# Two attention layers in one step loop: one row of maxima per quad, scores three steps behind

## The chip, the cores and the metric

One core of one Trainium2 chip. The metric is the time of one execution in device microseconds, the median of the runs shown; a change of some 0.2% is about the least that can be told.

## The reference, cut to what matters

Eight batches of 256 tokens with 256 features go through four layers, each added to x: cross-attention with a mask (called A here), a quantised linear layer, cross-attention with a bias and a feed-forward part (called C here), and a mixture of eight experts. Both attentions have 16 heads of 16 features; keys and values come from a context that is the same for A and C.

```python
x = x + _L0_xattn_ref(_layernorm(x), ctx, ctx, mask, W, b)          # A: scores, mask, softmax, values, W
x = x + _L0_ffn_ref(_layernorm(x), weight)                          # hadamard, 4-bit activations, ternary weight
x = x + _L1_xattn_ref(_layernorm(x), ctx, bias, Wq, Wk, Wv, ...)    # C: softmax(q k / 4 + bias) v, Wo, gelu FFN
x = x + _L1_ffn_ref(_layernorm(x) ..., Wr, W1, b1, W2, b2)          # top-k experts
```

The softmax is exact in form: the largest score of each row is taken away before the exponential.

## The kernel before, in words

**Quads.** The 16 heads of a batch are worked in four *quads* of four heads, of kind A or C. A quad's scores are 4 heads x 256 x 256. It has two *halves* of two heads. Each half is computed twice on TensorE, since the maximum has to be known first: once with queries along the partitions (`pe_maximum_scores`, L435, into the PSUM tile `row_scores`), of which VectorE takes the maximum of each row (`ve_take_maximum`, L646: one reduction for A, four fused add-and-maximum instructions with the bias for C), and once with keys along the partitions (`pe_scores`, L451, into `key_scores`), ready for the product with the values. Between the two, the maxima are laid into `row_max`, transposed on TensorE (`pe_maximum_rows`, L502, one pair of 128x128 transposes for each half, into `ps_r`) and added by VectorE to spare rows of the query operand (`ve_add_maximum`, L665, 64 partitions for each half), so that the second product gives scores with the maximum taken away. For A the mask is put in by two matmuls ahead of each product (`pe_mask`, L456). For C VectorE adds the bias to `key_scores` into `probs` (`ve_add_bias`, L677). ScalarE then takes the exponentials (`ac_exponentials`, L832), GpSimd sums blocks (`po_sum_blocks`, L968), and after both quads of a *chunk* TensorE forms the values and the row sums (`pe_values`, L511, into `ps_v`), which VectorE divides (`ve_normalise`, L687).

**Order of the work.** `timetable` (L52) puts each quad at a position. From the third batch on, A quads of batch b stand at even positions and C quads of batch b - 2 at odd ones, so A and C alternate; the first two batches have A quads alone, and the last two C quads stand side by side. Each position has two *steps*, one for each half, and a batch has 16 steps. In step 2p + h every engine does, in its own order: the maxima of half h of the quad at p + 1 (`then`), the scores of half h of the quad at p (`now`), the transposes and the add for the maxima of the step before, at h = 1 the values and the division of the quad before (where it ends a chunk), then the side jobs that a table puts at that step. Both products of a step are woven into one *round* (`pe_round`, L459): the two halves use different 32-row strips of the array (`group`, L372), so four matmuls run side by side. A round waits for the maxima of the step before to be taken (one `row_scores`), for `key_scores` to be read (by ScalarE for A, by VectorE for C) and for `max_added` of the half whose scores it forms. Where both quads are C, the two products go one behind the other (`pe_scores_apart`, L483); in this timetable that is so in the last two batches alone.

**Side jobs.** `PE_SLOT`, `VE_SLOT`, `AC_SLOT`, `PO_SLOT` (L87 to L96) give the step of each other piece of a batch, relative to 16 b; `move` (L106 to L121) overrides them for single batches. The names: T_x transposes a LayerNorm result, wa/wo the output products of A and C, had, T_q, tern the quantised layer, wk, wq, wv the projections of C, f1_n and f2_n the feed-forward parts, lg the router's logits; on VectorE st and ap are the LayerNorm statistics and their application, on GpSimd rs the reciprocal root, on ScalarE g0, g1 the gelus. The engines are in order; semaphores join them. SyncE's queue issues all loads in one loop over positions (L1465).

```python
for step in range(2 * FIRST, 2 * LAST):
    pos, half = divmod(step, 2)
    now, then, past = quad_of(pos), quad_of(pos + 1), quad_of(pos - 1)
    maximised, of_half = previous_half(step)
```

After the attention steps come the router (VectorE, `ve_route`, `ve_threshold`) and the eight experts.

## Time and profile before

| | |
|---|---|
| median of 3 runs | 979.02 us (977.69 to 979.81) |
| profiled execution | 979.38 us, its span 977.6 us |
| granted TensorE clock, mean | 0.921 |
| PE, DVE, ACT, POOL busy | 86%, 68%, 40%, 47% of the span |
| attention steps | first round at 13.67 us, last logits of the last batch copied at 712.59 us |

PE is TensorE's matmuls, PEld its weight loads, DVE VectorE, ACT ScalarE, POOL GpSimd, SP SyncE. Busy time of PE is modelled at its ends, so two neighbours can overlap by some 0.1 us; the distance from start to start is exact. A gap in square brackets is idle time of that engine ahead of the instruction, with what ended it.

### The profile page before, as it was taken

Reading aid. Unit: us, or ns where it says so; the run is one execution under the profiler, and the core shown is the slowest. Engines: PE = TensorE matmul, PEld = TensorE weight load, DVE = VectorE, ACT = ScalarE, POOL = GpSimd, SP = SyncE. Lnnn points to the kernel's source line nnn. Section 1 sums busy time; section 2 is a strip of 40 time slices with the busy share of each in tenths; the row PEclk is TensorE's granted clock in tenths of the full one; section 3 lists DMA queues with packets and bytes.
Section 4 is the critical chain, followed back from the end, with each engine's and each line's share of the span. In section 5 each row is a group of like instructions: output and inputs, shape, how many; then the busy total and the mean of one; then the engine's idle time right before and its main releaser. Section 6 shows DMA issues by size and latency. Waiting matters only on the chain.

```text
span 977.6 us, 17867 instructions
## 1 busy us (share of the span) xinstructions
PE 841.3 (86%) x7077; PEld 608.6 (62%) x7077; DVE 663.2 (68%) x1501; ACT 387.9 (40%) x594; POOL 456.9 (47%) x403
## 2 busy tenths in 40 slices
PE   6888877989999999999999979998733499999995
PEld 4555444545665665665665656666622399999985
DVE  4664468787798798798698687683266466666441
ACT  1322122324624624624524413423110266666662
POOL 4444234544536536536435334152320467777742
PEclk9998789989999999999999978989955599999998
DMA  9320543443443443443443335240050135545531
GB/s 288 123 61 12 199 167 131 141 150 109 149 164 117 160 168 115 161 168 112 159 140 112 127 129 195 91 148 11 33 183 0 44 114 130 135 130 130 135 71 22
DMA packets 47696, 120.57 MB, mean 123 GB/s; under 512 B 4736, under 2 KB 33920, under 8 KB 39424
## 3 DMA queue, kind: packets, MB, share of 16 engines
q1 hardware_dynamic: 41472, 111.06, 33.5%
q0 software_dynamic: 6144, 8.39, 4.8%
q8 instruction: 56, 0.92, 0.4%
q14 instruction: 24, 0.20, 0.1%
HBM read 111.05 MB, written 8.39 MB: 122 GB/s over the span
## 4 chain that ended last, share of the span: by engine, by line
PE 59%; DVE 21%; issue 7%; POOL 6%; ACT 4%; DMA 1%; POOLq 0%; SPq 0%; DVEq 0%
PE row_scores L437 9%; PE ps_v L525 8%; PE row_scores L1289 5%; PE ps_m L543 4%; PE ps_v L1306 4%; PE ps_r L1306 4%; DVE probs L683 3%; DVE row_max L653 3%; PE ps_v L407 3%; PE ps_m L414 3%; PE ps_r L507 2%; DVE attnT_C L692 2%; PE key_scores L457 2%; PE key_scores L1289 2%; PE ps_m L535 2%
## 5 line engine op out<-in xcount | busy, mean ns | idle before, releaser
L972 POOL TENSOR_TENSOR probs<-probs 128x512 f32<-128x512 f32 x128 | 162.0, 1272 | 112.2 <-ACT probs L841 89.4
L841 ACT ACTIVATE probs<-probs 128x1024 f32<-128x1024 f32 x64 | 67.7, 1057 | 233.1 <-DVE probs L683 233.0
L660 DVE CUSTOM_DVE_ANT_0 row_scores<-row_scores,bias_q 128x256 f32<-128x256 f32 x256 | 100.6, 453 | 38.3 <-PE row_scores L437 38.1
L838 ACT ACTIVATE probs<-key_scores 128x1024 f32<-128x1024 f32 x64 | 65.6, 1025 | 125.6 <-PE key_scores L453 124.9
L653 DVE TENSOR_REDUCE row_max<-row_scores 128x4 f32<-128x1024 f32 x64 | 78.1, 1221 | 48.3 <-PE row_scores L437 48.2
L683 DVE TENSOR_TENSOR probs<-key_scores,bias_k 128x1024 f32<-128x1024 f32 x64 | 77.8, 1215 | 7.5 <-PE key_scores L453 7.3
L437 PE MATMUL row_scores<-k_op_a,q_op_A 32*128 32x256 f32 x512 | 77.1, 420 | 6.4 <-DVE q_op_C L669 5.9
L437 PE MATMUL row_scores<-k_op_c,q_op_C 32*128 32x256 f32 x512 | 75.3, 413 | 4.9 <-DVE row_max L660 4.9
L453 PE MATMUL key_scores<-q_op_C,k_op_c 32*128 32x256 f32 x512 | 77.9, 424 | 0.4 <-DVE q_op_C L669 0.4
L453 PE MATMUL key_scores<-q_op_A,k_op_a 32*128 32x256 f32 x512 | 74.8, 411 | 0.0
L1371 POOL TENSOR_TENSOR w_l<-w1e,w_h 128x512 fp32r<-128x512 f32 x32 | 52.4, 1668 | 42.6 <-ACT w_h L1322 42.6
L1239 DVE TENSOR_TENSOR hid_l<-hid_e,hid_h 128x512 fp32r<-128x512 f32 x64 | 44.3, 692 | 40.8 <-ACT hid_e L1340 40.8
L437 PEld LDWEIGHTS row_scores<-k_op_a,q_op_A 32*128 32x128 f32 x512 | 47.1, 193 | 37.4 <-issue 22.0
L1380 POOL DMA_INDIRECT out<-y_g,idx x32 | 54.0, 1688 | 28.0 <-ACT y_g L1354 18.2
L437 PEld LDWEIGHTS row_scores<-k_op_c,q_op_C 32*128 32x128 f32 x512 | 45.0, 189 | 32.5 <-issue 17.9
L543 PE MATMUL ps_m<-w,hidT 128*128 128x256 f32 x256 | 61.0, 381 | 0.0
L1363 POOL DMA_INDIRECT xg<-normed_dram,idx x32 | 37.5, 1171 | 49.6 <-DVE idx L1213 36.0
L507 PE MATMUL ps_r<-ident,row_max 128*128 128x128 f32 x256 | 58.4, 311 | 0.0
L457 PE MATMUL row_scores<-mask_bf,ident_b 128*128 128x512 bf16 x128 | 40.1, 397 | 19.4 <-DVE row_max L653 11.0
L507 PEld LDWEIGHTS ps_r<-ident,row_max 128*128 128x128 f32 x256 | 26.6, 145 | 46.0 <-issue 46.0
L543 PEld LDWEIGHTS ps_m<-w,hidT 128*128 128x128 f32 x256 | 47.4, 190 | 6.6 <-issue 0.8
L453 PEld LDWEIGHTS key_scores<-q_op_C,k_op_c 32*128 32x128 f32 x512 | 46.9, 194 | 4.9 <-issue 2.4
(242 smaller groups left out, 2160.0 us busy)
## 6 DMA issues: line engine op xcount, KB each, us to landing
bias_q<-in_bias_q SPq DMA_DIRECT2D x32, 1024.0 KB, 5.0
bias_k<-in_bias_k SPq DMA_DIRECT2D x32, 1024.0 KB, 5.0
w1e<-in_w1e SPq DMA_DIRECT2D x8, 1024.0 KB, 5.1
w2e<-in_w2e SPq DMA_DIRECT2D x8, 1024.0 KB, 6.7
k_op_a<-in_k_a SPq DMA_DIRECT2D x32, 128.0 KB, 2.3
mask_int<-in_mask SPq DMA_DIRECT2D x8, 512.0 KB, 5.7
v_op_A<-in_v_a SPq DMA_DIRECT2D x8, 512.0 KB, 5.4
w<-in_w SPq DMA_DIRECT2D x2, 1024.0 KB, 10.4
```

Of the source, the lines that this page charges most:

```text
L437: return nc.tensor.matmul(row_scores[:, j % 2, qt * SEQ:(qt + 1) * SEQ], queries(q)[r, qt * P:(qt + 1) * P], keys(q)[r, :], start=(q.kind ...
L453: return nc.tensor.matmul(key_scores[:, j % 2, kb * SEQ:(kb + 1) * SEQ], keys(q)[r, kb * P:(kb + 1) * P], queries(q)[r, :], start=(q.kind ...
L507: ins = nc.tensor.matmul(ps_r[:, qt * P:(qt + 1) * P], row_max[q.par][MAX_TILE[q, half]][:, qt, :], ident[:, :], start=True, stop=True, is ...
L525: ins = nc.tensor.matmul(bank[32 * j:32 * j + 32, col:col + SEQ], left, probs[:, (first, last)[par] % 4, j, kb, :], start=(par == 0 and kb ...
L543: ins = nc.tensor.matmul(ps_m[1][:, t * D:(t + 1) * D], hidT[:, hc, t * P:(t + 1) * P], w_2[:, hc, :], start=(t == 0 and hc == 0), stop=(l ...
L653: nc.vector.tensor_reduce(of, row_scores[:, :, :].rearrange("p j (t k) -> p j t k", t=QT), AX_X, ALU.max).then_inc(max_taken, 1)
L660: ins = nc.vector.tensor_tensor_reduce(row_scores[:, j, qt * SEQ:(qt + 1) * SEQ], row_scores[:, j, qt * SEQ:(qt + 1) * SEQ], bias_q[:, m % ...
L683: nc.vector.tensor_tensor(probs[:, n % 4, heads(q, half), :, :].rearrange("p j t q -> p j (t q)"), key_scores[:, :, :], bias_k[:, m % 2, h ...
L841: nc.scalar.activation(of, of, ACT.Exp).then_inc(exp_done, 1)
L972: nc.gpsimd.tensor_tensor(both[:, :, 0, :], both[:, :, 0, :], both[:, :, 1, :], ALU.add).then_inc(blocks_summed, 1)
L1289: ins = nc.tensor.matmul(ps_h[hc % 3][:, :], w[:, c, cols_h], xT[:, c, :], start=(n == 0), stop=(n == 3 * DC - 1))
L1306: ins = nc.tensor.matmul(ps_e[i][:, (st % 2) * D:(st % 2 + 1) * D], hid[:, hc, st * P:(st + 1) * P], w[:, hc, :], start=(n == 0), stop=(n ...
```

## The change: what it does

Maxima stay where they are (`maximised_at`: the quad at p + 1 in steps 2p and 2p + 1). The transposes and the add are made once for a whole quad, in the even step after both its halves (`rows_at`); `row_max` has two tiles for each parity in place of three. The scores of a quad at p come at steps 2p + 1 and 2p + 2 (`scored_at`), one step later than before, and the values one step later (`valued_at`, always at an even step). Halves are strips 0 and 1 for every quad. C with C goes as a whole round except in the last two batches. The side jobs get new steps; in the tail every one is a step later.

```diff
-MAX_TILE = {(q, half): (2 * [p for p in ORDER if p.par == q.par].index(q) + half) % 3 for q in ORDER for half in range(2)}
...
 def values_step(kind, b, c):
-    return 2 * values_place(kind, b, c) + 1
-PE_SLOT = {"wb": -5, "wa": 0, "T_A": -32, "wv": 18, "wo": 35, "T_B": 3, "had": 4, "T_F": 39, "T_q": 6, "tern": 8, "f1_0": 40,
-           "T_R": 58, "f1_1": 42, "lg": 59, "f1_2": 43, "wk": 12, "T_C": 13, "f1_3": 45, "wq": 14,
-           "f2_0": 46, "f2_1": 50, "f2_2": 52, "f2_3": 53, "f2_4": 53, "f2_5": 53, "f2_6": 54, "f2_7": 54}
-VE_SLOT = {"wb0": -10, "wb1": -9, "wb2": -8, "wb3": -7, "stA": -35, "mask": -32, "apA": -34, "x1": 0, "apB": 2, "y": 35,
-           "quant": 4, "qcap": 5, "apF": 37, "yf": 54, "apG": 55, "yq": 8, "stR": 56, "apR": 57, "stC": 10, "apC": 11,
-           "lgc": 59}
-AC_SLOT = {"wb": -5, "qA": -32, "vC": 18, "hbT": 3, "zT": 39, "qT": 6, "xrT": 58, "g0": 42, "kC": 12, "xcT": 13, "g1": 45,
-           "qC": 14}
-PO_SLOT = {"rsA": -35, "xb": -34, "rsB": 0, "rsF": 35, "yb": 37, "rsG": 54, "aff": 55, "x2": 8, "rsR": 56, "rsC": 10,
-           "xe": 12, "mk": -21}
+    return 2 * PLACE[Quad(kind, b, 2 * c + 1)] + 4
+PE_SLOT = {"wb": -4, "wa": 1, "T_A": -30, "wv": 19, "T_B": 4, "had": 5, "wo": 38, "T_F": 41, "T_q": 7, "tern": 8, "f1_0": 43,
+          "wk": 11, "f1_1": 44, "T_C": 13, "f1_2": 45, "wq": 14, "f1_3": 46, "T_R": 63, "lg": 64,
+           "f2_0": 47, "f2_1": 49, "f2_2": 51, "f2_3": 52, "f2_4": 52, "f2_5": 53, "f2_6": 54, "f2_7": 55}
+VE_SLOT = {"wb0": -10, "wb1": -9, "wb2": -8, "wb3": -7, "stA": -35, "mask": -32, "apA": -34, "x1": 1, "apB": 3,
+           "quant": 5, "qcap": 6, "y": 38, "yf": 55, "apF": 39, "yq": 9, "apG": 57, "stR": 59, "stC": 11, "apC": 12, "apR": 61,
+           "lgc": 65}
+AC_SLOT = {"wb": -4, "qA": -30, "vC": 19, "hbT": 4, "zT": 41, "qT": 7, "kC": 11, "g0": 44, "xcT": 13, "qC": 14, "g1": 46,
+           "xrT": 63}
+PO_SLOT = {"rsA": -35, "xb": -34, "rsB": 1, "rsF": 38, "yb": 39, "rsG": 55, "x2": 9, "aff": 57, "rsR": 59, "rsC": 11,
+           "xe": 13, "mk": -20}
...
-move(0, stA=-32, rsA=-32, apA=-31, xb=-31, T_A=-30, qA=-30, wa=2, x1=2, rsB=2, apB=2, T_q=5, qT=5, qcap=4, tern=6, yq=6,
...
+move(0, stA=-32, rsA=-32, apA=-31, xb=-31, T_A=-30, qA=-30, wa=3, x1=3, rsB=3, apB=3, T_B=4, hbT=4, had=5, quant=5, qcap=5,
...
-move(4, f2_0=111, f2_1=111, f2_2=112, f2_3=112, f2_4=112, f2_5=113, f2_6=113, f2_7=113, yf=114, rsG=114, apG=115, aff=115,
...
+move(4, f2_0=112, f2_1=112, f2_2=113, f2_3=113, f2_4=113, f2_5=114, f2_6=114, f2_7=114, yf=115, rsG=115, apG=116, aff=116,
...
-        row_max = [[lay(f"row_max_{par}{n}", [P, QT, P]) for n in range(3)] for par in range(2)]
+        row_max = [[lay(f"row_max_{par}{n}", [P, QT, P]) for n in range(2)] for par in range(2)]
...
-        def group(quad, half):
-            return (PLACE[quad] - 1 + half) % 2
-
-        def previous_half(step):
-            pos, half = divmod(step - 1, 2)
-            return quad_of(pos + 1), half
+        def maximised_at(step):
+
+            return quad_of(step // 2 + 1), step % 2
+
+        def scored_at(step):
+            return quad_of((step - 1) // 2), (step - 1) % 2
+
+        def rows_at(step):
+            return quad_of(step // 2) if step % 2 == 0 else None
+
+        def valued_at(step):
+            q = quad_of(step // 2 - 2) if step % 2 == 0 else None
+            return q if q is not None and q.par == 1 else None
...
             nc.tensor.matmul(bank, ident_b[:, :], mask_bf[:, q.b % 2, way, :], start=True, stop=False)
 
-        def pe_round(pe, now, then, half):
+        def pe_round(pe, now, of_now, then, of_then):
             if then is not None:
-                pe_wait_maximum(pe, then, half)
+                pe_wait_maximum(pe, then, of_then)
                 if then.kind == A:
                     for n in range(2):
                         pe_mask(row_scores[:, n, :], then, 0)
             if now is not None:
-                pe_wait_scores(pe, now, half)
+                pe_wait_scores(pe, now, of_now)
                 if now.kind == A:
                     for n in range(2):
                         pe_mask(key_scores[:, n, :], now, 1)
-                pe.wait_ge(max_added, half_number(now, half) + 1)
+                pe.wait_ge(max_added, number(now) + 1)
...
-        def pe_maximum_rows(pe, q, half):
-            n = half_number(q, half)
-            pe.wait_ge(max_taken, n + 1)
-            wait(pe, max_added, n)
+        def pe_maximum_rows(pe, q):
+            pe.wait_ge(max_taken, 2 * number(q) + 2)
+            wait(pe, max_added, number(q))
             for qt in range(QT):
-                ins = nc.tensor.matmul(ps_r[:, qt * P:(qt + 1) * P], row_max[q.par][MAX_TILE[q, half]][:, qt, :], ident[:, :],
+                ins = nc.tensor.matmul(ps_r[:, qt * P:(qt + 1) * P], row_max[q.par][MAX_TILE[q]][:, qt, :], ident[:, :],
                                        start=True, stop=True, is_transpose=True)
...
             for step in range(2 * FIRST, 2 * LAST):
-                pos, half = divmod(step, 2)
-                now, then, past = quad_of(pos), quad_of(pos + 1), quad_of(pos - 1)
-                maximised, of_half = previous_half(step)
-                if now is not None and then is not None and now.kind == then.kind == C:
-                    pe_scores_apart(pe, now, then, half)
+                (now, of_now), (then, of_then) = scored_at(step), maximised_at(step)
+                if now is not None and then is not None and now.kind == then.kind == C and now.b >= NB - 2:
+                    pe_scores_apart(pe, now, of_now, then, of_then)
                 elif now is not None or then is not None:
-                    pe_round(pe, now, then, half)
-                if maximised is not None:
-                    pe_maximum_rows(pe, maximised, of_half)
-                if half == 1 and past is not None and past.par == 1:
-                    pe_values(pe, past)
+                    pe_round(pe, now, of_now, then, of_then)
+                if rows_at(step) is not None:
+                    pe_maximum_rows(pe, rows_at(step))
+                if valued_at(step) is not None:
+                    pe_values(pe, valued_at(step))
                 for job, b in due(PE_SLOT, step):
...
 
-        def ve_add_maximum(ve, q, half):
-            g = group(q, half)
-            r = slice(64 * g, 64 * g + 64)
-            ve.wait_ge(max_rows, half_number(q, half) + 1)
-            nc.vector.tensor_tensor(queries(q)[r, :], ps_r[r, 0:SEQ], queries(q)[r, :], ALU.add).then_inc(max_added, 1)
+        def ve_add_maximum(ve, q):
+            ve.wait_ge(max_rows, number(q) + 1)
+            nc.vector.tensor_tensor(queries(q), ps_r[:, 0:SEQ], queries(q), ALU.add).then_inc(max_added, 1)
...
         def heads(q, half):
-            return slice(2 * group(q, half), 2 * group(q, half) + 2)
+            return slice(2 * half, 2 * half + 2)
...
             nc.gpsimd.tensor_tensor(v[:, :, 1, :], v[:, :, 1, :], v[:, :, 0, :], ALU.subtract).then_inc(v_parted[kind], 1)
 
         def po_previous(po, step):
-            pos, half = divmod(step - 1, 2)
-            q = quad_of(pos)
+            q, half = scored_at(step - 1)
             if q is not None:
                 po_sum_blocks(po, q, half)
                 if q.w == 1 and half == 0:
...
         def po_start(po):
             nc.gpsimd.memset(half_neg[:, :], -0.5).then_inc(S["const_done"], 1)
             for par in range(2):
-                for n in range(3):
+                for n in range(2):
                     nc.gpsimd.memset(row_max[par][n][:, :, :], 0.0).then_inc(S["const_done"], 1)
             nc.gpsimd.memset(v_op[C][:, :, :, :], 0.0).then_inc(S["const_done"], 1)
-            po.wait_ge(S["const_done"], 8)
+            po.wait_ge(S["const_done"], 6)
         ps_h = [row_scores[:, 0, :], row_scores[:, 1, :], key_scores[:, 0, :]]
         ps_c = key_scores[:, 1, :]
```

The waits for the constants fall from 8 to 6 with the two memsets, `T_R` of the last batch waits for as many adds as there are quads, and ScalarE and VectorE use the same four functions as `pe_layers`.

## Rows read from the trace of the kernel before

**Rows 1.** Page, busy us, share of the span and instructions of each engine.
```profile
PE 841.3 (86%) x7077; PEld 608.6 (62%) x7077; DVE 663.2 (68%) x1501; ACT 387.9 (40%) x594; POOL 456.9 (47%) x403
```

**Rows 2.** Windows by batch: length, busy PE PEld DVE ACT POOL, clock, DMA, GB/s.
```profile
185.38:260.11 74.73, 67.80 (x621) 42.24 (x620) 58.34 (x140) 31.89 (x43) 34.80 (x32) 0.93 0.40 138
...
333.65:407.20 73.55, 70.50 (x662) 47.28 (x661) 62.18 (x154) 32.25 (x44) 39.08 (x38) 1.00 0.44 148
...
480.74:553.11 72.37, 69.32 (x638) 46.70 (x637) 59.01 (x145) 31.02 (x43) 34.58 (x34) 1.00 0.42 145
```

**Rows 3.** Waits of PE, 333.65 to 407.20: us in total, times, longest.
```profile
PE ps_m L399 <- DVE nrm_R L709: 1.1, 1, 1.1
PE ps_m L535 <- ACT hidT L858: 0.9, 1, 0.9
```

**Rows 4.** Timeline of PE, parts of 366 to 403: start, us, what.
```profile
366.49 1.93 PE L525 MATMUL ps_v<-probs,v_op_A 128*32 128x256 f32 x32
...
369.21 0.66 PE L399 MATMUL ps_m<-ident,nrm_AF 128*128 128x128 f32 x4
369.70 0.59 PE L457 MATMUL key_scores<-mask_bf,ident_b 128*128 128x512 bf16 x2
...
398.02 0.48 PE L437 MATMUL row_scores<-k_op_a,q_op_A 32*128 32x256 f32 x2
...
399.09 0.44 PE L507 MATMUL ps_r<-ident,row_max 128*128 128x128 f32 x2
...
399.37 1.89 PE L414 MATMUL ps_m<-hbT,w_q 128*128 128x256 f32 x8
...
401.10 1.03 PE L543 MATMUL ps_m<-w,hidT 128*128 128x256 f32 x4
...
401.96 0.59 PE L457 MATMUL row_scores<-mask_bf,ident_b 128*128 128x512 bf16 x2
...
402.48 0.48 PE L437 MATMUL row_scores<-k_op_a,q_op_A 32*128 32x256 f32 x2
```

**Rows 5.** Timeline of PE at 65, two mask pairs ahead of a round.
```profile
65.06 0.59 PE L457 MATMUL row_scores<-mask_bf,ident_b 128*128 128x512 bf16 x2
...
66.02 0.48 PE L437 MATMUL row_scores<-k_op_a,q_op_A 32*128 32x256 f32 x2
```

**Rows 6.** Timeline, DVE behind rounds, and PE behind DVE.
```profile
381.26 0.73 DVE L709 TENSOR_SCALAR nrm_R<-x_all,mv_R,rstd_R 128x256 f32<-128x256 f32 x2
...
382.13 0.63 PE L399 MATMUL ps_m<-ident,nrm_R 128*128 128x128 f32 x4 [1.09 <-DVE nrm_R L709]
...
386.03 1.23 DVE L653 TENSOR_REDUCE row_max<-row_scores 128x4 f32<-128x1024 f32 x1 [0.26 <-PE row_scores L437]
...
387.17 1.21 DVE L683 TENSOR_TENSOR probs<-key_scores,bias_k 128x1024 f32<-128x1024 f32 x1
...
388.41 0.43 DVE L669 TENSOR_TENSOR q_op_A<-ps_r,q_op_A 64x256 f32<-64x256 f32 x1
...
390.37 0.48 PE L437 MATMUL row_scores<-k_op_c,q_op_C 32*128 32x256 f32 x2
...
391.55 0.43 DVE L660 CUSTOM_DVE_ANT_0 row_scores<-row_scores,bias_q 128x256 f32<-128x256 f32 x1 [1.65 <-PE row_scores L437]
...
393.05 0.41 DVE L669 TENSOR_TENSOR q_op_A<-ps_r,q_op_A 64x256 f32<-64x256 f32 x1
```

**Rows 7.** Groups of PE, 333.65 to 407.20: busy us, mean ns, idle before.
```profile
L507 PE MATMUL ps_r<-ident,row_max 128*128 128x128 f32 x32 | 7.0, 301 | 0.0
```

**Rows 8.** Timeline of POOL at the start.
```profile
4.49 1.63 POOL L1040 MEMSET row_max<- 128x256 f32 x6
```

**Rows 9.** Timeline of DVE, a chunk's division.
```profile
369.42 1.76 DVE L692 RECIPROCAL attnT_A<-ps_v 128x256 f32<-128x256 f32 x1
```

**Rows 10.** A gap of PE (timeline), then the window after it (columns as rows 2).
```profile
211.57 0.60 PE L457 MATMUL row_scores<-mask_bf,ident_b 128*128 128x512 bf16 x2 [2.67 <-DVE row_max L660]
...
212.80:223.00 10.20, 9.30 (x73) 4.36 (x70) 6.08 (x8) 2.59 (x3) 5.68 (x5) 0.50 0.33 107
```

More of the change, by code:

```diff
@@ L117 @@
-move(7, wa=112, x1=112, rsB=112, apB=112, T_B=113, hbT=113, had=114, quant=114, qcap=114, T_q=115, qT=115, tern=116, yq=116,
-     x2=116, stC=117, rsC=117, apC=117, T_C=118, xcT=118, wq=119, qC=119, xe=118, wk=120, kC=120, wv=124, vC=124, wo=134,
-     y=134, rsF=134, apF=135, yb=135, T_F=136, zT=136, f1_0=137, f1_1=137, f1_2=137, f1_3=137, g0=137, g1=137, f2_0=138,
-     f2_1=138, f2_4=139, f2_5=139, f2_2=140, f2_3=140, f2_6=141, f2_7=141, yf=141, rsG=141, apG=142, aff=142, stR=143,
-     rsR=143, apR=144, T_R=145, xrT=145, lg=146, lgc=146)
+move(4, f2_0=112, f2_1=112, f2_2=113, f2_3=113, f2_4=113, f2_5=114, f2_6=114, f2_7=114, yf=115, rsG=115, apG=116, aff=116,
+     stR=118, rsR=118, apR=119, T_R=122, xrT=122, lg=123, lgc=123)
@@ new lines @@
+move(5, wo=115, y=115, rsF=115, apF=116, yb=116, T_F=118, zT=118, f1_0=119, f1_1=121, g0=121, f1_2=122, f1_3=123, g1=123,
+     f2_0=125, f2_1=125, f2_2=126, f2_3=126, f2_4=127, f2_5=127, f2_6=128, f2_7=128, yf=128, rsG=128, apG=129, aff=129,
+     stR=130, rsR=130, apR=131, T_R=132, xrT=132, lg=133, lgc=133)
+move(6, wv=117, vC=117, wo=125, y=125, rsF=125, apF=126, yb=126, T_F=129, zT=129, f1_0=130, f1_1=131, g0=131, f1_2=132,
+     f1_3=133, g1=133, f2_0=134, f2_1=134, f2_2=134, f2_3=134, f2_4=135, f2_5=135, f2_6=135, f2_7=135, yf=136, rsG=136,
+     apG=137, aff=137, stR=138, rsR=138, apR=139, T_R=140, xrT=140, lg=141, lgc=141)
@@ new lines @@
+move(7, wa=113, x1=113, rsB=113, apB=113, T_B=114, hbT=114, had=115, quant=115, qcap=115, T_q=116, qT=116, tern=117, yq=117,
+     x2=117, stC=118, rsC=118, apC=118, T_C=119, xcT=119, wq=120, qC=120, xe=119, wk=121, kC=121, wv=125, vC=125, wo=135,
+     y=135, rsF=135, apF=136, yb=136, T_F=137, zT=137, f1_0=138, f1_1=138, f1_2=138, f1_3=138, g0=138, g1=138, f2_0=139,
+     f2_1=139, f2_4=140, f2_5=140, f2_2=141, f2_3=141, f2_6=142, f2_7=142, yf=142, rsG=142, apG=143, aff=143, stR=144,
+     rsR=144, apR=145, T_R=146, xrT=146, lg=147, lgc=147)
@@ L481, in pe_round, with pe_scores_apart @@
                 ins_now.then_inc(scores_ready, 1)
-        def pe_scores_apart(pe, now, then, half):
-            pe_wait_maximum(pe, then, half)
+        def pe_scores_apart(pe, now, of_now, then, of_then):
+            pe_wait_maximum(pe, then, of_then)
             if then.kind == A:
@@ L488, in pe_scores_apart @@
             for t in range(QT):
-                for j in heads_of(group(then, half)):
+                for j in heads_of(of_then):
                     ins_then = pe_maximum_scores(then, j, t)
             ins_then.then_inc(max_scores, 1)
-            pe_wait_scores(pe, now, half)
+            pe_wait_scores(pe, now, of_now)
             if now.kind == A:
@@ L640, in pe_layers @@
                     pe_keep_busy(24, ps_m[1])
-                if -11 <= step <= 8 and step != -5:
+                if -11 <= step <= 8 and step != -4:
                     pe_keep_busy(8, ps_m[1])
@@ L649, in ve_take_maximum @@
             first = DK * (1 - q.par)
-            g = group(q, half)
-            of = row_max[q.par][MAX_TILE[q, half]][:, :, :].rearrange("p t (j r) -> p j t r", j=4)[:, 2 * g:2 * g + 2, :, first]
+            g = half
+            of = row_max[q.par][MAX_TILE[q]][:, :, :].rearrange("p t (j r) -> p j t r", j=4)[:, 2 * g:2 * g + 2, :, first]
             if q.kind == A:
@@ L815, in ve_layers @@
             for step in range(2 * FIRST, 2 * LAST):
[L816 to L818 removed]
+                (now, of_now), (then, of_then) = scored_at(step), maximised_at(step)
                 if then is not None:
[L820 removed]
+                    ve_take_maximum(ve, then, of_then)
                 if now is not None and now.kind == C:
[L822 to L826 removed]
+                    ve_add_bias(ve, now, of_now)
+                if rows_at(step) is not None:
+                    ve_add_maximum(ve, rows_at(step))
+                if valued_at(step) is not None:
+                    ve_normalise(ve, valued_at(step))
                 for job, b in due(VE_SLOT, step):
@@ L915, in ac_layers @@
             for step in range(2 * FIRST, 2 * LAST):
-                pos, half = divmod(step, 2)
-                now = quad_of(pos)
+                now, of_now = scored_at(step)
                 if now is not None:
-                    ac_exponentials(ac, now, half)
+                    ac_exponentials(ac, now, of_now)
                 for job, b in due(AC_SLOT, step):
```

38 lines of the change are left out of this document (11 added, 27 removed).

## Prediction

> **What bounds the kernel now.** I read the page's table of engines first: TensorE (PE) is busy for 86% of the span, VectorE (DVE) for 68% [rows 1]. Both are averages over a start, a steady stretch of attention, a tail and the experts, so next I cut the span into batches of sixteen steps, at the starts of their first rounds [rows 2]. Five batches, from 185.38 to 553.11 us, are nearly alike: in the one from 333.65 PE is busy for 70.50 of 73.55 us at the full clock, DVE for 62.18. The change touches the steps of the attention only; what follows them is the same work.
>
> In that batch PE idles 3.05 us, and the table of its waits names LayerNorm and gelu as the longest, not the scores [rows 3]. Measured from start to start I find 4.1 us of waiting (T_R 1.3, f1_2 1.0, w_a 0.6, values 0.4, six of 0.05 to 0.3); the difference lies under the modelled ends of matmuls. So PE's own list is 73.55 - 4.1 = 69.4 us: today this list sets the batch, and DVE's results mostly come in time.
>
> **Prices on PE, start to start** [rows 4]. A round 1.07 us (398.02 to 399.09); one pair of transposes of maxima 0.28 (to 399.37); a product of eight matmuls 1.73; a part of f2 0.86; a pair of masks with the change to the round 0.52; the values of a chunk 2.72; four transposes 0.49. Two mask pairs take 0.96 to the round [rows 5], so a pair alone 0.44 and the change of tile shape some 0.1, which a round without masks pays after its predecessor. Each is paid in full, for the next instruction follows at once.
>
> **Prices on DVE** [rows 6]. DVE starts 1.18 us after a round's start (390.37 to 391.55). Maxima of a C half take 1.50, of an A half 1.14, adding the bias 1.24, adding the maxima to the queries 0.43. PE starts 0.14 us after DVE's end (381.99 to 382.13).
>
> **Removed: half of the transposes.** A batch has 32 transposes, 16 pairs [rows 7]; eight pairs go: 8 x 0.28 = 2.24 us of PE's list, which becomes 67.2. On DVE eight adds of 0.43 go, 3.4 us; DVE has 11 us to spare in the batch, so this is worth nothing by itself. An add over 128 partitions does not stand in the trace: between 0.43 (as long in the free axis) and 0.86 (twice the data), I take 0.43, the nearest row. Two of the six memsets at the start go, a third of 1.63 us [rows 8]: -0.5 us.
>
> The starts after the transposes follow without a gap [rows 4], so the sum takes the 2.24 in full. The Trainium skill ("Perfetto Trace Analysis", Identifying the Most-Contended Engine) speaks against this: it would judge TensorE's headroom by the share of weight loads, not of matmuls. By that rule PE has room, as weight loads fill 47.28 of 73.55 us [rows 2], the removal gives nothing, and the time is that of rival 3, 1002.
>
> **Moved: which halves meet in a round.** Scores now come three steps behind maxima. At odd steps an A and a C half still share a round, but at even steps two A halves meet, or two C halves. The chain from round to round through DVE changes; call a step by its number modulo four:
>
> - before, scores of C with maxima of A: 1.18 + 1.14 + 1.24 + 0.43 + 0.14 = 4.13 (twice in four steps); scores of A with maxima of C: 1.18 + 1.50 + 0.14 + 0.52 = 3.34 (twice). Sum 14.94.
> - after, step 0 (C with C): 1.18 + 1.50 + 1.24 + 0.14 + 0.52 = 4.58, since the masks of A wait for the bias to leave key_scores; step 1: 1.18 + 1.50 + 0.14 + 0.96 = 3.78; step 2 (A with A): 1.18 + 1.14 + 0.14 + 0.52 = 2.98; step 3: 1.18 + 1.14 + 1.24 + 0.14 = 3.70, since the whole round of C with C waits for maxima and bias both. Sum 15.04.
>
> So where only this chain binds, the start up to 185 us, I cost the move at nothing. In a full batch it matters what PE has to do meanwhile. Values and transposes now all stand at even steps; odd steps keep side jobs alone. With the new slots, for steps 64 to 79, PE's list from round to round against the chain:
>
> - step 68: 1.07 + 0.28 + 0.49 + 2 x 0.86 + 0.52 = 4.08 against 4.58: 0.50 short
> - step 71: 1.07 + 0.2 (T_q, four transposes in bf16, an estimate below the 0.49) + 0.86 + 0.1 = 2.25 against 3.70: 1.45
> - step 73: 1.07 + 0.49 (T_F) + 0.96 = 2.52 against 3.78: 1.26
> - step 76: 1.07 + 0.28 + 1.73 + 0.52 = 3.60 against 4.58: 0.98
> - step 79: 1.07 + 0.49 + 0.86 + 0.1 = 2.52 against 3.70: 1.18
>
> The other eleven are longer than their chain (step 74: 1.07 + 0.28 + 2.72 + 0.52 = 4.59 against 2.98); time spare there cannot be lent to another step, as row_scores and key_scores have one buffer each. Together 5.4 us.
>
> **Queued behind.** DVE works in order. At step 72 it normalises (a reciprocal of 1.76 us [rows 9] and more) ahead of the maxima of step 73, and comes to step 72 itself late from four LayerNorm jobs: I estimate 1.5 us in the batch, between 0 and 2.2. f1_2 still waits for gelu, 0.9 us before [rows 3], 1.0 taken. Behind gelu ScalarE reloads its table ahead of the exponentials that step 78's masks wait for: 0.8, between 0 and 1.3, an estimate. In all 5.4 + 1.5 + 1.0 + 0.8 = 8.7 us of waits in place of 4.1.
>
> **Other jobs.** wo, T_F, f1, T_R, lg and their DVE, ScalarE and GpSimd parts run one to five steps later in the batch, in the same order on each bank; nobody in the steady stretch needs them within that time, so I cost them at nothing; without that cover it is one step. The SP queue's loads of keys and bias_k, released by scores and bias, are released one step later and needed one step later or, for the keys, some ten steps off: nothing, else one landing of about 5 us in the stretch where C follows C.
>
> **The tail.** Values and every last job run one step later: one step more, 73.55 / 16 = 4.6 us, between 3 and 6.
>
> **Sum.** A batch: 67.2 + 8.7 = 75.9, against 73.55: +2.35, five times +11.8. Tail +4.6, memsets -0.5. The profiled execution took 979.38 us (span 977.6), 0.4 above the median of 979.02: 979.4 + 11.8 + 4.6 - 0.5 = 995. Bounds: without the estimates of lateness (6.4 us of waits) a batch is 73.6 and the kernel 983.7; with 3.05 instead of 4.1 us of waits in the list before, a batch is 77.0 and the kernel 1001.
>
> **Rivals.**
>
> 1. *PE's list stays the bound* (the other side). If the chains of steps 71, 73, 76 and 79 are covered as those of before are, waits stay near 4.1 and five batches lose 11.2 us: 979.4 - 11.2 + 4.6 - 0.5 = 972. It decides at 6.3 us of waits in a batch: below that a batch is faster. For it: DVE has 3.4 us less to do. Against it: the chains above are bare sums of rows in which DVE does nothing else, and step 71 has 2.25 us of list to set against 3.70. Chance 0.13.
> 2. *The clock falls too.* Before, an idle gap of 2.67 us on PE was followed by half the clock from 212.8 to 223.0 [rows 10], while the batches after 223 us, with gaps of 1.1, ran at 1.00. After, step 73 leaves PE idle for some 2 us in every batch. One fall costs between 1.2 us (the batch from 185.38 against that from 333.65) and 5 (half of 10.2); I take 2.2, as many have short falls: five times 2.2 gives 1006. Chance 0.19.
> 3. *The transposes give nothing back.* Of the eight pairs, the three at steps 71, 73 and 79 are under the chain in my sum already; if the other five are too, a batch gains 1.4 us more: 995 + 7 = 1002. The rows speak against it. Chance 0.05.
> 4. *Nothing changes*: waits near 6.3, with the tail's step offset by a shorter start: 979 within 2 us. That the change does less than it says, I exclude: the pairs are gone by the loop. Chance 0.05.
>
> **Numbers.** Forecast 995, chance 0.58; its own range 983 to 1003. Slower by over 0.2%, about 2 us, which is what a measurement of this kernel can tell: 0.58 + 0.19 + 0.05 = 0.82; the same 0.05; faster 0.13. The range from 978 to 1012 takes in rivals 2 to 4 and leaves out rival 1.
>
> **What would show it.** In the changed kernel: batches of about 75.9 us with PE idle 7 to 9 us; at rounds two and four of each four, waits of 1 to 2 us on the bias (probs) or on the maxima (row_max), the longest ahead of the two mask pairs of step 74; 16 transposes of maxima in a batch instead of 32; the logits of the last batch some 15 us later. I am wrong if batches are under 73.5 us, if the waits stand on other tiles, or if the granted clock differs between 223 and 550 us.

## Result and the profile after

The changed kernel takes 999.91 us (median of 4 runs, 998.35 to 1001.94), the kernel before 978.36 (median of 4 runs): 1.0236 times as long, 95% interval 1.021 to 1.0261. The forecast was 995 us, range 978 to 1012, with a chance of 0.82 that it is slower. The sign and the range are right; the median lies 5 us above the forecast.

The page after, its busy times, against [rows 1]:

```profile
span 997.0 us, 17404 instructions
## 1 busy us (share of the span) xinstructions
PE 824.7 (83%) x6896; PEld 596.4 (60%) x6949; DVE 636.4 (64%) x1437; ACT 387.5 (39%) x594; POOL 457.2 (46%) x401
```

PE and DVE both do less than before, in a longer span: time has gone into waiting. The windows say where. The first fence is the kernel before from the first round of step 32 to that of step 112, and from there to the last copy of logits; the second is the changed kernel in the same two stretches, then its batch of steps 64 to 79, which answers to [rows 2] (columns: length, busy time of PE, PEld, DVE, ACT and POOL with instructions, PE's clock, DMA share, GB/s).

```profile
185.38:553.11 367.73, 348.59 (x3238) 230.76 (x3237) 302.32 (x737) 159.63 (x217) 184.48 (x173) 0.99 0.42 145
553.11:712.59 159.48, 136.56 (x941) 100.78 (x940) 95.19 (x270) 47.44 (x73) 51.08 (x57) 0.89 0.27 97
```

```profile
182.99:562.64 379.65, 335.54 (x3106) 219.99 (x3145) 286.95 (x696) 157.59 (x216) 184.19 (x172) 0.99 0.40 138
562.64:732.57 169.93, 141.13 (x996) 104.31 (x996) 94.56 (x264) 51.01 (x77) 53.50 (x59) 0.88 0.27 97
...
336.49:412.46 75.97, 68.19 (x636) 45.39 (x645) 59.70 (x145) 32.23 (x45) 39.28 (x37) 1.00 0.43 143
```

The span is 19.4 us longer. The start is 2.4 shorter (182.99 against 185.38), the five batches are 11.9 longer (379.65 against 367.73), the tail 10.4 (169.93 against 159.48), and behind the last logits 0.6 is gained. In the batch PE is busy 2.3 us less than before but idle for 7.8, against 3.05, at the full clock. Its waits there, where [rows 3] named LayerNorm and gelu:

```profile
engine line waited for: us in total, times, longest us
PE key_scores L464 <- DVE probs L685: 1.7, 3, 1.0
PE row_scores L464 <- DVE row_max L664: 1.7, 1, 1.7
PE row_scores L444 <- issue: 1.2, 1, 1.2
PE row_scores L444 <- DVE probs L685: 1.2, 1, 1.2
PE ps_m L541 <- ACT hidT L858: 0.9, 1, 0.9
PE key_scores L464 <- ACT probs L838: 0.6, 1, 0.6
```

Most are waits of masks (L464) or rounds (L444) for DVE's bias (probs) or maxima (row_max), the tiles that the prediction named; the two for hidT and for ScalarE's probs are gelu's. PE's timeline shows them where steps 68, 71, 73, 76 and 79 end, the steps that it found short:

```profile
360.13 0.38 PE L464 MATMUL key_scores<-mask_bf,ident_b 128*128 128x512 bf16 x1 [0.34 <-DVE probs L685]
...
373.27 0.48 PE L444 MATMUL row_scores<-k_op_c,q_op_C 32*128 32x256 f32 x2 [1.24 <-issue]
...
382.14 0.60 PE L464 MATMUL row_scores<-mask_bf,ident_b 128*128 128x512 bf16 x2 [1.65 <-DVE row_max L664]
...
396.80 0.38 PE L464 MATMUL key_scores<-mask_bf,ident_b 128*128 128x512 bf16 x1 [1.01 <-DVE probs L685]
...
412.46 0.48 PE L444 MATMUL row_scores<-k_op_c,q_op_C 32*128 32x256 f32 x2 [1.19 <-DVE probs L685]
```

The profile names no releaser for the wait at 373.27 ("issue"). DVE's timeline has the end of a bias add 0.09 us before it (371.96 + 1.22 = 373.18), so I count it as a wait for the bias too:

```profile
371.96 1.22 DVE L685 TENSOR_TENSOR probs<-key_scores,bias_k 128x1024 f32<-128x1024 f32 x1
```

### The profile page after: what moved, and what is told of

It is laid out like the page before. It is cut to its first block, busy times and chain, and to the rows that moved or that the text cites. A ratio compares the mean times of both kernels' runs of the same rounds, so it can differ in the third digit from the quotient of the medians.

```text
span 997.0 us, 17404 instructions
## 1 busy us (share of the span) xinstructions
PE 824.7 (83%) x6896; PEld 596.4 (60%) x6949; DVE 636.4 (64%) x1437; ACT 387.5 (39%) x594; POOL 457.2 (46%) x401
## 4 chain that ended last, share of the span: by engine, by line
PE 58%; DVE 22%; issue 8%; ACT 5%; DMA 4%; POOL 3%; SPq 0%; POOLq 0%; DVEq 0%; ACTq 0%
PE row_scores L444 10%; PE ps_v L531 8%; PE row_scores L1287 5%; PE ps_m L549 4%; DVE probs L685 4%; PE ps_v L1304 3%; PE ps_r L1304 3%; DVE row_scores L664 3%; PE ps_v L414 3%; PE ps_m L414 3%; DVE row_max L657 3%; PE row_scores L464 2%; PE key_scores L464 2%; PE ps_m L421 2%; DMA bias_q<-in_bias_q 2%
## 5 line engine op out<-in xcount | busy, mean ns | idle before, releaser
L444 PE MATMUL row_scores<-k_op_c,q_op_C 32*128 32x256 f32 x512 | 78.9, 427 | 32.5 <-issue 12.0
L444 PEld LDWEIGHTS row_scores<-k_op_c,q_op_C 32*128 32x128 f32 x512 | 47.8, 196 | 58.4 <-issue 34.1
L460 PE MATMUL key_scores<-q_op_A,k_op_a 32*128 32x256 f32 x512 | 78.1, 425 | 0.0
L444 PE MATMUL row_scores<-k_op_a,q_op_A 32*128 32x256 f32 x512 | 77.2, 421 | 0.0
L444 PEld LDWEIGHTS row_scores<-k_op_a,q_op_A 32*128 32x128 f32 x512 | 46.2, 194 | 31.1 <-issue 29.0
L464 PE MATMUL row_scores<-mask_bf,ident_b 128*128 128x512 bf16 x97 | 32.7, 393 | 27.2 <-DVE row_max L657 12.9
L464 PE MATMUL key_scores<-mask_bf,ident_b 128*128 128x512 bf16 x106 | 35.5, 402 | 19.5 <-DVE probs L685 13.7
L460 PEld LDWEIGHTS key_scores<-q_op_A,k_op_a 32*128 32x128 f32 x512 | 46.6, 196 | 1.9 <-issue 1.7
```

Of the source, the lines that this page charges most:

```text
L444: return nc.tensor.matmul(row_scores[:, j % 2, qt * SEQ:(qt + 1) * SEQ], queries(q)[r, qt * P:(qt + 1) * P], keys(q)[r, :], start=(q.kind ...
L460: return nc.tensor.matmul(key_scores[:, j % 2, kb * SEQ:(kb + 1) * SEQ], keys(q)[r, kb * P:(kb + 1) * P], queries(q)[r, :], start=(q.kind ...
L464: nc.tensor.matmul(bank, ident_b[:, :], mask_bf[:, q.b % 2, way, :], start=True, stop=False)
```

## The experiments

**An extra pair of transposes, in the kernel before.** The forecast took 0.28 us for each pair removed.

```diff
-            for qt in range(QT):
+            for qt in 2 * list(range(QT)):
                 ins = nc.tensor.matmul(ps_r[...], row_max[...][:, qt, :], ident[:, :], ...)
```

> The kernel before, with every pair of transposes of maxima issued twice (the same two matmuls into the same bank). Theory (each pair costs 0.28 us of TensorE's own list, which binds): a batch has 16 pairs, +4.5 us, less up to 1 us where TensorE waits anyway: 77.0 to 78.1 us for a batch of 73.55, and 999 to 1015 us for the kernel, since the start and the tail have pairs too (128 x 0.28 = 36 us at the most). Rival (transposes give nothing back, as they stand beside waits or weight loads): 979 to 982 us, batches of 73.6. On VectorE the only effect is 0.28 us of lateness for the add behind each pair.

Measured: 982.2 us, 1.0066 times before (1.0044 to 1.0089; each ratio is against the kernel before, run beside it), and batches of 75.30 us, +1.76:

```profile
329.79:405.09 75.30, 72.82 (x686) 50.84 (x693) 61.99 (x154) 32.40 (x44) 39.06 (x38) 1.00 0.42 145
```

Neither side had it right. The timeline of PE shows the end of a round, the four transposes, then the values:

```profile
362.67 0.38 PE L453 MATMUL key_scores<-q_op_C,k_op_c 32*128 32x256 f32 x2
362.98 0.66 PE L507 MATMUL ps_r<-ident,row_max 128*128 128x128 f32 x4
363.56 1.93 PE L525 MATMUL ps_v<-probs,v_op_A 128*32 128x256 f32 x32
```

With four, the group takes 0.66, where two take 0.44 (7.0 us for 16 pairs) [rows 7]: 0.22 for an extra pair right behind another. That is not the price of a lone pair, which stays at 0.28: in the kernel before a side job starts 1.35 us after its round where a pair stands between (398.02 to 399.37) [rows 4], in the changed kernel 1.08 where none does (408.67 to 409.75). From the starts of the rounds, step by step: eight of the sixteen steps grew by 0.21 to 0.22, two by 0.07 and 0.08, five by nothing, and step 73 shrank by 0.14. So already before the change half of the steps were not set by PE's list alone; the 4.1 us of waits that the forecast had found lie in ten places.

The kernel's median lost 5.4 us, less than five times 1.76. In the profiled execution the five batches grew by 6.1 us together (the first of them, from step 32, shrank by 0.66, at a mean granted clock of 0.98 in place of 0.93), and the start went the other way. These windows are from the first round to the first round of step 32, before and with the pairs twice:

```profile
13.67:185.38 171.71, 140.39 (x1300) 84.45 (x1299) 111.35 (x223) 46.63 (x58) 73.50 (x64) 0.90 0.38 130
```

```profile
14.41:180.42 166.01, 138.24 (x1349) 88.24 (x1365) 110.28 (x223) 46.77 (x58) 73.72 (x64) 0.95 0.38 132
```

With more work PE passes this stretch 5.7 us sooner, at a mean granted clock of 0.95 in place of 0.90.

**The same in the changed kernel.** All else stays as changed; a batch has 16 pairs again.

```diff
-            for qt in range(QT):
+            for qt in 2 * list(range(QT)):
                 ins = nc.tensor.matmul(ps_r[...], row_max[q.par][MAX_TILE[q]][:, qt, :], ident[:, :], ...)
```

> The changed kernel with its pairs of transposes issued twice, so that a batch has 16 pairs again as before the change, all else as changed. It asks what the removal of eight pairs is worth where it now stands. In the kernel before, an extra pair cost 0.22 us at each of nine steps of sixteen and nothing at the others. Theory: the eight pairs stand at even steps, of which two (68 and 76) are set by the chain and cover them; the other six cost 0.2 to 0.28 each: a batch takes 77.2 to 77.6 in place of 75.96, the kernel 1002 to 1008 us. Rival (the transposes give nothing back, now that DVE's chain sets the batch): 75.9 to 76.2, 997 to 1002 us.

Measured: 1004.43 us, 1.0277 (1.0226 to 1.0328).

```profile
336.59:413.66 77.07, 69.75 (x653) 47.13 (x661) 59.74 (x145) 32.24 (x45) 39.29 (x37) 1.00 0.41 141
```

77.07 - 75.97 = 1.10 us, just under the expected 77.2 to 77.6 (the steps that paid before were eight, not nine as the expectation says). The table of the next experiments shows why: five of the eight even steps grow by 0.22, and 68, 72 and 76 by nothing. So eight pairs put back where the pairs now stand cost 1.1 us in a batch, and by that figure the other parts of the change cost 2.43 + 1.10 = 3.5. The pairs that the change removed stood alone at odd steps, and no run puts them back there. By the next experiments three of the eight odd steps are set by their list and three are not, and two were not tried; at 0.28 for each that pays, I estimate 0.8 to 1.4 us.

**Filling the waits, and filling the full steps.** Sixteen small matmuls into a free bank at the end of a step, first at steps whose list was found short of their chain, then at steps whose list was longer.

```diff
+                if 32 <= step < 112 and step % 16 in (7, 9, 15):     # the other kernel: (1, 5, 11)
+                    pe_keep_busy(16, ps_r)
```

> The changed kernel with 16 small extra matmuls (48 of them took 2.8 us, so 0.93 us) at the end of steps 7, 9 and 15 of each sixteen, from step 32 to 111: the steps where the working found TensorE's list 1.2 to 1.5 us short of the chain through VectorE. Theory (those steps are set by the chain): the extra work fits into the waits, a batch of 75.96 grows by 0 to 0.5 us, the kernel takes 999 to 1003 us, and TensorE is 2.8 us busier in the batch. Rival (the list sets every step, or the clock or a queue does): +2.8 us a batch, 1014 us.

> The changed kernel with the same 16 extra matmuls at the end of steps 1, 5 and 11 of each sixteen, steps whose list is longer than their chain. Theory: nothing covers them, a batch of 75.96 grows by 2.2 to 2.8 us, the kernel takes 1010 to 1014 us. Rival (the chain through VectorE sets the whole batch, and TensorE has room everywhere): under +0.5 us a batch, 999 to 1003 us.

Measured: 995.72 us, 1.0195 (1.0154 to 1.0236), and 1013.87 us, 1.0379 (1.0343 to 1.0414). The same batch, the waits filled, then the full steps:

```profile
330.53:406.50 75.97, 70.88 (x684) 48.30 (x693) 59.69 (x145) 32.24 (x45) 39.30 (x37) 1.00 0.42 143
```

```profile
338.01:416.66 78.65, 70.88 (x685) 48.16 (x693) 59.17 (x145) 32.24 (x45) 39.37 (x37) 1.00 0.40 138
```

The first kernel ended below its range of 999 to 1003 us. In the execution that was profiled its start took 166.37 us and its first batch 75.23, where the changed kernel's took 169.97 and 77.57, both at a higher mean clock (0.91 against 0.88, 0.98 against 0.93); up to step 32 the two kernels are the same (last section). So here the batch at the full clock is compared. PE is busy for 70.88 us in both, 2.7 more than in the changed kernel. In the one the batch is 75.97 us long, as without it; in the other 78.65. Step by step, from the start of one round to the next in the timelines (us):

| step | before | after | waits filled | full steps filled | after, pairs twice |
|---|---|---|---|---|---|
| 64 | 4.72 | 5.61 | 5.61 | 5.61 | 5.83 |
| 65 | 4.71 | 4.73 | 4.73 | **5.62** | 4.73 |
| 66 | 4.68 | 5.19 | 5.19 | 5.19 | 5.41 |
| 67 | 4.19 | 3.86 | 3.86 | 3.86 | 3.86 |
| 68 | 4.47 | 4.57 | 4.56 | 4.56 | 4.57 |
| 69 | 4.47 | 4.73 | 4.73 | **5.62** | 4.73 |
| 70 | 4.14 | 4.47 | 4.47 | 4.47 | 4.69 |
| 71 | 5.19 | 3.64 | **3.64** | 3.64 | 3.64 |
| 72 | 4.18 | 5.48 | 5.48 | 5.48 | 5.48 |
| 73 | 5.11 | 4.35 | **4.35** | 4.35 | 4.35 |
| 74 | 5.33 | 4.71 | 4.71 | 4.71 | 4.93 |
| 75 | 5.52 | 4.73 | 4.73 | **5.62** | 4.73 |
| 76 | 3.60 | 4.56 | 4.56 | 4.56 | 4.56 |
| 77 | 4.04 | 6.23 | 6.23 | 6.23 | 6.23 |
| 78 | 4.47 | 5.33 | 5.33 | 5.33 | 5.55 |
| 79 | 4.71 | 3.79 | **3.79** | 3.79 | 3.79 |

The filled steps are in bold. Steps 71, 73 and 79 take 0.9 us of extra work each for nothing; 65, 69 and 75 pay 0.89 for it. In these six steps, then, a step is set either by its list or by its chain, and time spare in one helps no other.

**C beside C apart.** One part of the change undone.

```diff
-                if now is not None and then is not None and now.kind == then.kind == C and now.b >= NB - 2:
+                if now is not None and then is not None and now.kind == then.kind == C:
                     pe_scores_apart(pe, now, of_now, then, of_then)
```

> The changed kernel with the scores of C beside C issued apart everywhere, as before the change, in place of whole rounds: maxima of the next quad first, then the scores. Theory (a whole round waits for maxima and bias both, apart only its second part waits for the bias): the start and the steady batches lose part of their waits, a batch takes 74.8 to 75.4 in place of 75.96, the kernel 992 to 997 us. Rival (the two halves in one round save TensorE as much as the wait costs): 998 to 1003 us, with waits moved from maxima to scores and batches of 75.8 to 76.5.

Measured: 1000.21 us, 1.0248 (1.0215 to 1.0282), batches of 75.75: nearly the rival's case.

```profile
331.76:407.51 75.75, 70.31 (x637) 46.63 (x644) 59.69 (x146) 32.25 (x45) 39.32 (x37) 1.00 0.42 143
```

The waits of the first round on the bias are gone from PE's table,

```profile
PE key_scores L464 <- DVE probs L685: 1.8, 3, 1.0
PE row_scores L464 <- DVE row_max L664: 1.7, 1, 1.7
PE ps_m L541 <- ACT hidT L858: 0.9, 1, 0.9
PE key_scores L464 <- ACT probs L838: 0.6, 1, 0.6
```

and the maxima of steps 72 and 80 start 1.2 us sooner (71 and 79 last 2.46 and 2.53 us), but those steps last about as much longer (72 takes 6.65, and 64, sixteen steps ahead of 80, 6.66). PE is busy 70.31 us in place of 68.19. The whole round is not what the change costs.

**Two side jobs moved.** In the changed kernel gelu stands ahead of the exponentials for which step 78 waits. ScalarE's timeline:

```profile
397.55 1.28 ACT L858 ACT_TABLE_LOAD   x1
398.84 0.84 ACT L858 ACTIVATE hidT<-ps_m,cols 128x256 f32<-128x256 f32 x2
399.57 0.84 ACT L858 ACTIVATE hidT<-ps_v,cols 128x256 f32<-128x256 f32 x2
400.43 1.28 ACT L838 ACT_TABLE_LOAD   x1
401.72 1.02 ACT L838 ACTIVATE probs<-key_scores 128x1024 f32<-128x1024 f32 x1
```

Two table loads of 1.28 us enclose the gelu. The Trainium skill ("ScalarE: Activation LUTs", What ACT_TABLE_LOAD costs) states 1283 ns for one; the trace agrees. The 1380 ns of drain that the section adds to a switch do not stand in this timeline, where the gelu starts 0.01 us behind the load. PE waits 0.89 for hidT and then 0.64 for probs, in step 77, the longest of the batch at 6.23 us.

```diff
-... "f1_3": 46 ... "g0": 44
+... "f1_3": 47 ... "g0": 43
```

> The changed kernel with two side jobs moved: the first gelu (g0, ScalarE) one step earlier, from step 12 to 11 of each sixteen, and f1_3 (TensorE, 1.73 us) one step later, from step 14 to 15, into a step whose list was short of its chain. Theory (waits at named steps set the batch, not the list): f1_3 fits into the 1.2 us that step 15 lacks, and steps 13 and 14 lose their waits for gelu and the exponentials; a batch takes 72.5 to 74 in place of 75.96, the kernel 983 to 991 us. Rival (the sum of PE's list sets the batch, so moving work within it is worth nothing): 75.5 to 76.5, and 998 to 1001 us.

Measured: 987.66 us, 1.0106 (1.0087 to 1.0124).

```profile
330.84:403.62 72.78, 67.74 (x637) 45.40 (x645) 60.18 (x145) 32.26 (x45) 39.28 (x37) 1.00 0.43 149
```

Step 77 falls from 6.23 to 4.26, step 78 from 5.33 to 3.61, and step 79 takes f1_3 in for 0.51: together -3.2 us a batch, with nearly the same work on every engine. The run makes both moves at once, but the steps keep them apart. Step 77 lost 1.97 with gelu's two waits, which no longer stand in PE's table. Step 78, without f1_3's eight matmuls, lost 1.72, about their price of 1.73, and step 79, which had been short, took them in for 0.51. A gelu that runs a step sooner delays the exponentials of a C half, for which PE's table shows no wait.

**The tail.** In the changed kernel a wait stands there that before did not. It stands in DVE's table of waits behind step 112; then DVE's timeline and the queue of SP:

```profile
DVE row_scores L664 <- DMA bias_q<-in_bias_q: 7.3, 2, 6.2
```

```profile
647.50 1.22 DVE L685 TENSOR_TENSOR probs<-key_scores,bias_k 128x1024 f32<-128x1024 f32 x1
648.64 0.42 DVE L671 TENSOR_TENSOR q_op_C<-ps_r,q_op_C 128x256 f32<-128x256 f32 x1
...
651.10 1.22 DVE L685 TENSOR_TENSOR probs<-key_scores,bias_k 128x1024 f32<-128x1024 f32 x1
658.51 0.43 DVE L664 CUSTOM_DVE_ANT_0 row_scores<-row_scores,bias_q 128x256 f32<-128x256 f32 x1 [6.19 <-DMA bias_q<-in_bias_q]
```

```profile
648.75 0.33 SPq L1430 DMA_DIRECT2D bias_k<-in_bias_k  x1
649.12 0.44 SPq L1438 DMA_DIRECT2D normed_dram<-nrm_R  x1
649.61 0.47 SPq L1427 DMA_DIRECT2D bias_q<-in_bias_q  x1
```

bias_k may be loaded once DVE has added the bias two C quads earlier, which the change makes a step later (the add ended at 648.72 us, 647.50 + 1.22). bias_q needs only the maxima of an earlier quad, and these come no later than before, but its load stands behind bias_k's on the queue. It is issued at 649.61 and used at 658.51.

```diff
             def load_bias(q):
...
                 sp.dma_start(bias_q[:, m % 2, :, :, :], ...)
+
+            def load_bias_k(q):
+                m = C_NUMBER[q]
                 if m >= 2:
                     sp.wait_ge(bias_added, 2 * (m - 2) + 2)
                 sp.dma_start(bias_k[:, m % 2, :, :, :], ...)
...
                 if ahead is not None and ahead.kind == C:
                     load_bias(ahead)
+                behind = quad_of(pos + 3)
+                if behind is not None and behind.kind == C:
+                    load_bias_k(behind)
```

> The changed kernel with each load of bias_k issued one place (two steps) later on the SP queue, so that where C follows C the next bias_q no longer stands behind the wait for bias_added. Theory (of the 10.4 us that the tail lost, one landing of some 5 us is bias_q queued behind bias_k): the 6.2 us wait of row_scores for bias_q in the tail goes, the stretch behind step 112 is 4 to 6 us shorter, steady batches stay at 75.96, the kernel takes 993 to 996 us. Rival (the landing is late for another reason, bandwidth or the lead of four places): the wait stays over 4 us, or turns up at bias_k, and the kernel takes 998 to 1001 us.

Measured: 990.81 us, 1.0137 (1.0117 to 1.0158), below the expected 993 to 996. The queue in the same place, where bias_q now goes first, and the tail's window:

```profile
645.74 0.33 SPq L1427 DMA_DIRECT2D bias_q<-in_bias_q  x1
652.21 7.69 SPq L1433 DMA_DIRECT2D bias_k<-in_bias_k  x2
```

```profile
563.85:729.82 165.97, 140.74 (x996) 103.52 (x996) 94.59 (x265) 51.13 (x77) 53.53 (x59) 0.89 0.28 99
```

No wait for bias_q is left in DVE's table. The tail takes 165.97 us in place of 169.93, 4.0 less, the low end of the expected 4 to 6; the steady stretch stays as it was (379.87). The median fell by more than that, some 9 us, and this is not explained. The execution that was profiled was the slowest of the six at 995.94, with a mean granted clock of 0.917; the other five had 0.920 to 0.927, the four of the changed kernel 0.917 to 0.919. So part may be the clock, for the tails of other executions with the old queue order took 170.8 to 175.1 us and the longest three, full steps filled, two side jobs moved and C apart, ran them at 0.84 and 0.85 of the clock.

**Versions that beat the kernel before.** If waits at single steps are the cost, both orders should give some back. First four slots of the kernel before, then the changed kernel with both mends and five more moves, then with eighteen:

```diff
 kernel before
-"T_A": -32 ... "xrT": 58 ... "g0": 42 ... "aff": 55
+"T_A": -33 ... "xrT": 57 ... "g0": 41 ... "aff": 56
 changed kernel, with bias_q ahead of bias_k
-"f1_3": 46 ... "g0": 44 ... "f2_1": 49 ... "f2_2": 51 ... "f2_6": 54 ... "stC": 11 ... "vC": 19
+"f1_3": 47 ... "g0": 43 ... "f2_1": 51 ... "f2_2": 52 ... "f2_6": 55 ... "stC": 9 ... "vC": 18
 changed kernel, with bias_q ahead of bias_k
-"wo": 38, "y": 38, "apF": 39, "T_F": 41, "zT": 41, "f1_0": 43, "f1_1": 44, "g0": 44, "f1_2": 45, "f1_3": 46, "g1": 46
+"wo": 36, "y": 36, "apF": 38, "T_F": 40, "zT": 40, "f1_0": 41, "f1_1": 43, "g0": 42, "f1_2": 44, "f1_3": 45, "g1": 45
-"f2_1": 49, "f2_4": 52, "f2_5": 53, "f2_6": 54, "stC": 11, "vC": 19, "mk": -20
+"f2_1": 47, "f2_4": 53, "f2_5": 54, "f2_6": 55, "stC": 9, "vC": 18, "mk": -22
```

> The kernel before with four slots moved by one step: g0 and xrT (ScalarE) and T_A (TensorE) earlier, aff (GpSimd) later. It asks whether the old order has waits to give back as well: by the working 4.1 us of a batch of 73.55 are waits, those at T_R 1.3 and gelu 1.0 the largest. Theory: a batch takes 71.5 to 72.5, the kernel 968 to 974 us. Rival (the old order's list is the bound): 73.3 to 73.7, 976 to 979 us.

> The changed kernel with the SP order of the first run of this call, the two moves of the second, and five more side jobs one or two steps off (f2_1, f2_2, f2_6 later, stC and vC earlier), each into a step that was short. Theory: one row of maxima per quad makes the list shorter than before (67.2 against 69.4 us), so with its waits covered a batch takes 71.5 to 73 us and the kernel 971 to 980 us, level with the kernel before or under it. Rival (three steps of distance cost as much whatever the side jobs do): over 75 us a batch, 990 us or more.

> The changed kernel with the SP order mended and eighteen side jobs moved by one or two steps, so that no step of the batch is much shorter than its chain: wo, y, T_F, the four f1 and both gelus earlier, four parts of f2 later. Theory: the list of 67 to 68 us plus the chain's remaining surplus gives a batch of 69.4 to 70.5 us in place of 75.96, the kernel 958 to 966 us, under both kernels and under the kernel before with its own moves (965.75). Rival (71.7 us, as in the last run, is what the distance of three steps allows): 968 to 973 us.

Measured: 965.75 us, 0.9884 (0.9859 to 0.9909), below its range; 970.74 us, 0.9936 (0.9918 to 0.9954), just below its range; 966.07 us, 0.9895 (0.9854 to 0.9936), 0.1 above its range. One batch of each, in this order:

```profile
324.15:396.74 72.59, 69.75 (x654) 47.29 (x661) 63.50 (x154) 32.13 (x44) 39.11 (x38) 1.00 0.45 150
```

```profile
322.68:394.38 71.70, 67.53 (x638) 45.50 (x645) 60.10 (x145) 32.24 (x45) 39.28 (x37) 1.00 0.43 152
```

```profile
320.74:391.55 70.81, 67.65 (x636) 45.46 (x645) 60.41 (x145) 32.16 (x45) 39.55 (x37) 1.00 0.45 153
```

The old order's batch of 72.59 us is 0.96 shorter than without its four moves. That is the smaller part of what it gained: in the profiled execution the span is 12.3 us shorter, of which the start has 5.2 (166.47 us, mean clock 0.92 in place of 0.90), the first batch 4.2 (70.55 us, 0.98 in place of 0.93) and the other four 3.7. Which of the moves shortened the start, or whether the clock alone did, was not tried.

The new order with eighteen moves has the shortest batch of all, 70.81 us, a little above the expected 69.4 to 70.5, and PE is idle for 3.2 us of it. It still only draws level with the old order and its four moves, since its tail from step 112 to the last logits is 7 us longer:

```profile
531.88:698.33 166.45, 141.50 (x996) 103.28 (x996) 94.59 (x265) 49.77 (x76) 53.60 (x59) 0.88 0.28 99
```

The old order was given four moves and the new one eighteen. Which order is the better one with its side jobs placed as well as can be is left open.

## Why the prediction was right, and where it was off

- **What bounds.** "PE's own list sets the batch" was too simple for the kernel before: an extra pair of transposes was paid in full at eight of sixteen steps.
- **Removed transposes: taken too high, by how much is open.** The forecast took 8 x 0.28 = 2.24 us off the list and gave part of it back in its own sum, since the short steps 71, 73 and 79 wait longer by what their list loses; by rival 3's count 1.4 us a batch were left. Pairs put back at the even steps cost 1.10, 0.22 each at five steps of eight; for the odd steps, from which they went, the estimate is 0.8 to 1.4. Rival 3, by which they give nothing back, does not hold for the even steps. The rule of the Trainium skill that the prediction set beside rival 3 ("Perfetto Trace Analysis", Identifying the Most-Contended Engine) would give nothing back (it names MFU beside the share of weight loads, of which the forecast took the latter alone); in the runs with pairs twice 1.10 us a batch came back, step by step, which no share over a batch tells.
- **Chain from round to round: right.** Steps 68, 71, 73, 76 and 79 were forecast at 4.58, 3.70, 3.78, 4.58 and 3.70 us and took 4.57, 3.64, 4.35, 4.56 and 3.79; the waits at their ends were forecast at 0.50, 1.45, 1.26, 0.98 and 1.18 and are 0.34, 1.24, 1.65, 1.01 and 1.19. Filling three of the steps cost nothing. Only step 73 is over, by 0.57; with a wait of 0.39 for the bias at the end of step 72 (378.45 in PE's timeline) that is some 1.0 us in the stretch for which 1.5 of DVE's lateness had been allowed. The add over 128 partitions takes 0.42 us (648.64 in DVE's timeline), the add over 64 took 0.43 [rows 6]: the nearest row was the right one.
- **Gelu and exponentials: right.** 1.0 and 0.8 us forecast, 0.89 and 0.64 in PE's timeline; moving gelu took both away, and step 77 was then 1.97 shorter.
- **A batch:** 75.9 forecast, 75.97 measured; five, +11.8 against +11.9. That it fits to 0.1 us is in part luck: DVE's lateness came out some 0.5 us below its allowance, gelu 0.2 above, and the pairs gave back up to 0.6 less than the forecast had left of them, so the errors cancel.
- **The tail: mis-sized.** Forecast +4.6 for one step, measured +10.4. The step that failed is that of the other jobs, "the SP queue's loads of keys and bias_k ... nothing, else one landing of about 5 us in the stretch where C follows C". The second value was the right one to take. I had named bias_k and not asked what is queued behind its wait: bias_q, whose use did not move. With the queue mended +6.5 is left (165.97 against 159.48). PE is busy 4.2 us longer in that window than before (140.74 against 136.56), about one step of work; the other 2 us are not explained. The logits of the last batch came 20.0 us later, where some 15 were forecast.
- **Start and memsets.** Four memsets take 1.13 us where six took 1.63, the 0.5 that was forecast. The whole start is 2.4 shorter, but this can't be told from chance: four executions with the same start reached step 32 between 179.4 and 183.7 us.
- **Rivals.** *PE's list stays the bound* fell with this choice of slots: 7.8 us of idle PE, above the 6.3 at which it decides. Its condition is what the runs with moved jobs bring about: at 3.2 us the batch is shorter than before. *The clock falls too* did not happen: 1.00 in the four batches behind the first, which has 0.93 before and after, and 0.99 over the whole stretch in both. *Nothing changes* is excluded by the interval.

## What to carry to other kernels

Where an engine's work is cut into steps by a single-buffered hand-over, compare its list with the chain of results at each step, not in the sum: removed work counts only in steps that the list sets, and extra work that fits into the wait is free in the others. A change of the distance between producer and consumer changes which steps these are, so the side jobs have to be placed anew with it; here that was worth 5 us a batch (75.97 to 70.81), and the removal itself about 1. When a release moves by a step, ask of each queue that waits for it what stands behind that wait, above all loads whose own time of need has not moved.
